# Two-layer adaLN block on one core: float32r products split in parts become plain float32 matmuls

## The chip, the cores and the metric

The kernel runs on one core of a Trainium2 chip. The metric is the device time of one execution in microseconds. Three timed runs of the kernel before took 1040.23, 1040.41 and 1041.82 us, so the median is 1040.41 us.

## The reference

Two layers follow each other on x, two batches of 1024 rows of 128 features. Each layer normalises x, scales and shifts it by a modulation, adds an attention, and then does the same with a feed-forward part. The change touches the second layer alone:

```python
h = layernorm(x) * (1 + ca) + sa
q, k, v = h @ Wq, h @ Wk, h @ Wv              # 128 -> 16 heads of 64
w = softmax(q @ k.T + position_bias)          # 2 batches x 16 heads, 1024 x 1024
x = x + ga * ((w @ v) @ Wo)
h = layernorm(x) * (1 + cb) + sb
for e in range(8):                            # two of eight experts chosen for each row
    inter = h @ wi.T + bi + (h @ lora_A[e].T) @ lora_B[e].T
    out += gate[e] * (relu(inter) @ wo.T + bo)
```

All of it is float32.

## The kernel before

The order of each engine's work is written out by hand; semaphores order the engines against each other. The first layer, its router and its eight experts take the first 200 us and are not touched.

**The second attention.** A unit u is one pair of heads of one batch: 8 pairs x 2 batches = 16 units of 8 tiles. A tile n is 128 query rows of both heads of the pair against 1024 keys; there are 128. Each engine runs through slots n (`pe_slot`, `act_slot`, `dve_slot`, `pool_slot`). In slot n TensorE does:

1. `pe_scores(n + 2)`: query times keys for both heads. The heads lie on partitions 0 to 63 and 64 to 127, so a matmul of one head takes 64 rows of the array and the other head's runs beside it;
2. `pe_turn(n, 0)`: 16 transposes of the softmax of the first head;
3. at most one chunk of the next unit's projections (`pe_chunk`): slots 0 to 3 hold the four chunks of q and k, slots 5 and 7 the two of v, slots 4 and 6 none (unit 1 has its own list, the last unit has four turns of weights instead);
4. `pe_values`: half of a group's product with v. A group is two tiles; the first head goes to partitions 0 to 63 of the bank and the second to 64 to 127, which are two column halves of the array;
5. `pe_turn(n, 1)`: 16 transposes of the second head;
6. in even slots from 4 on `pe_wo`, the output projection of a group.

VectorE adds the position bias to the scores and takes the row bound in one custom instruction for each head (L516), copies the second turn out (L524), and scales the output projection (L533). ScalarE takes the exponentials (L482), copies the first turn out (L474) and each projection chunk (L289, L298). GpSimd adds the result to x (L557, L560).

**The split.** TensorE multiplies q, k and their inputs as float32r (fp32r), one instruction a product. So that the result stays precise, each operand is kept as a high part (its cast to float32r) and a low part (the rest), and each product is made of three matmuls that add up in the bank: high x high, low x high, high x low. This holds for the q and k projections (L354), the scores (L372) and, in the feed-forward part, the products with wi (`base`, L1329) and lora_B (L1363). The parts have to be made:

- h: a cast on ScalarE (L760, `h_high`) and a difference on VectorE (L1045, `split_h`) or, for the second batch, on GpSimd (L710);
- q and k: ScalarE writes `raw_qk`, GpSimd casts (L322) and subtracts (L324); in unit 0 VectorE subtracts (L307);
- the weights: GpSimd (L565, L567);
- the feed-forward part: GpSimd splits its weights (L717, L718) and h (L723, L724), VectorE the low-rank product (L1104) and its masked copies (L1110, L1111).

Every other product is plain float32, which the trace shows as two MATMUL instructions for each matmul of the program (L406: 1024 in the program, 2048 in the trace).

**Getting into the second attention.** The experts' output is gathered in four quarters; VectorE makes x and the normalised rows of each, TensorE turns them (`turn_rows(2, k)`), ScalarE writes `hT`. Unit 0's chunks, and the scores of tiles 0 to 3, are laid between these by hand.

**The feed-forward part** takes 4 steps k of 512 rows: `base` (4 matmuls), two masked products `j` (8 matmuls; 24 instructions as split), the next step's low-rank product and mask turns (`choices`), and 16 output matmuls (L1373).

Of the kernel before, what the change touches and what calls it, by code (L numbers as in the profile page):

```python
# [15 lines left out]
F32R = mybir.dt.float32r  # L16
# [48 lines left out]
def build(nc, rel_hot, L0_attn_x, L0_attn_Wq, L0_attn_bq, L0_attn_Wk, L0_attn_bk, L0_attn_Wv, L0_attn_bv,  # L65
# [4 lines left out]
    with ExitStack() as ctx:  # L70
# [18 lines left out]
        h_high = sb("h_high", [P, N], F32R)  # L89
        h_low = sb("h_low", [P, N], F32R)  # L90
        h_parts = (h_high, h_low)
# [7 lines left out]
        w_parts = sb("w_parts", [P, 2, 2, CK], F32R)  # L99
# [8 lines left out]
        raw_qk = sb("raw_qk", [P, 2, CK])  # L108
        wo_out = sb("wo_out", [P, 2, 2, 2, D])
        qk0 = sb("qk0", [P, 4, S], F32R)  # L110
        with nc.sbuf_tensor("probsT", [P, 2, 2, TB, P], F32) as probsT:
            pass
        qk1 = sb("qk1", [P, 4, S], F32R)
        qk = (qk0, qk1)
        V1 = sb("V1", [P, 2, TB, P])
        wpair = sb("wpair", [P, 2, 3, P])
        wsplit = sb("wsplit", [P, 2, 2, 2, P], F32R)
# [38 lines left out]
        h_ffn = [qk0[:, 0:2, :].rearrange("p a n -> p (a n)"), qk0[:, 2:4, :].rearrange("p a n -> p (a n)")]  # L156
        lowrank = [part(h_high, 0, 512), part(h_high, 512, 512)]
        masked = h_low[:, :].rearrange("p (j a n) -> p j a n", j=2, a=2)

        passes = ((0, 0), (1, 0), (0, 1))  # L160
# [121 lines left out]
        def act_chunk(act, u, c):  # L282

            kind, q = chunk_of(u, c)
            act.wait_ge(ev("proj_full"), 6 * u + c + 1)
            if kind == "v":
                if u >= 2:
                    act.wait_ge(ev("pv_done"), 4 * (u - 1))
                act.copy(V1[:, u % 2, 4 * q:4 * q + 4, :].rearrange("p t d -> p (t d)"), chunk_bank(u, c)).then_inc(ev("high_out"), 1)  # L289
                return  # L290
            sign = -1.0 if kind == "q" else 1.0
            if u == 0:
                act.mul(qk[0][:, 0 if kind == "q" else 2, q * CK:(q + 1) * CK], chunk_bank(u, c), sign).then_inc(ev("high_out"), 1)
                return

            if 4 * u + c >= 6:
                act.wait_ge(ev("low_out"), 4 * u + c - 1)
            act.mul(raw_qk[:, c % 2, :], chunk_bank(u, c), sign).then_inc(ev("high_out"), 1)  # L298

        def dve_chunk(dve, u, c):  # L300

            kind, q = chunk_of(u, c)
            if kind == "v":
                return
            k = 0 if kind == "q" else 2
            dve.wait_ge(ev("high_out"), 6 * u + c + 1)
            dve.scalar_tensor_tensor(out=qk[u % 2][:, k + 1, q * CK:(q + 1) * CK], in0=chunk_bank(u, c),  # L307
                                     scalar=-1.0 if kind == "q" else 1.0,
                                     in1=qk[u % 2][:, k, q * CK:(q + 1) * CK].bitcast(F32),
                                     op0=ALU.mult, op1=ALU.subtract).then_inc(ev("low_out"), 1)  # L310

        def pool_chunk(pool, u, c):

            kind, q = chunk_of(u, c)
            if kind == "v":
                return
            k = 0 if kind == "q" else 2
            at = slice(q * CK, (q + 1) * CK)
            pool.wait_ge(ev("high_out"), 6 * u + c + 1)
            if u >= 2:  # L320
                pool.wait_ge(ev("scores"), 2 * TB * (u - 1))
            pool.tensor_copy(qk[u % 2][:, k, at], raw_qk[:, c % 2, :]).then_inc(ev("qk_high"), 1)  # L322
            pool.wait_ge(ev("qk_high"), 4 * (u - 1) + c + 1)
# [522 lines left out]
        def _(dve):  # L846
# [207 lines left out]
            for c in range(2):  # L1054
                dve_chunk(dve, 0, c)
# [345 lines left out]
```

## Time and profile before

| | |
|---|---|
| median of the three timed runs | 1040.41 us |
| the profiled execution | 1039.06 us |
| its span from first to last instruction | 1037.3 us |
| TensorE matmul busy | 934.1 us, 90% |
| VectorE busy | 668.4 us, 64% |
| ScalarE busy | 590.0 us, 57% |
| GpSimd busy | 281.7 us, 27% |

Busy time counts the union of an engine's instructions. Matmuls are pipelined: the recorded length of one is longer than the time until the next can start, so what a stage costs TensorE is read from the starts. The span is the profiled execution's own time less 1.76 us that lie around it.

### The profile page before, as it was taken

Reading aid. Unit: us, or ns where it says so; the run is one execution under the profiler, and the core shown is the slowest. Engines: PE = TensorE matmul, PEld = TensorE weight load, DVE = VectorE, ACT = ScalarE, POOL = GpSimd, SP = SyncE. Lnnn points to the kernel's source line nnn. Section 1 sums busy time; section 2 is a strip of 40 time slices with the busy share of each in tenths; the row PEclk is TensorE's granted clock in tenths of the full one; section 3 lists DMA queues with packets and bytes.
Section 4 is the critical chain, followed back from the end, with each engine's and each line's share of the span. In section 5 each row is a group of like instructions: output and inputs, shape, how many; then the busy total and the mean of one; then the engine's idle time right before and its main releaser. Section 6 shows DMA issues by size and latency. Waiting matters only on the chain. (4 is left out here: it accounts for less than half of the span.)

```text
span 1037.3 us, 24542 instructions
## 1 busy us (share of the span) xinstructions
PE 934.1 (90%) x9958; PEld 687.5 (66%) x9958; DVE 668.4 (64%) x1352; ACT 590.0 (57%) x980; POOL 281.7 (27%) x332
## 2 busy tenths in 40 slices
PE   7888349457999999999999999999999999996897
PEld 6467338345777777677777767777777776774786
DVE  6277401285767777677677777667777776774665
ACT  2533113236666766766766676676667667672343
POOL 1100540332341422324233142333414233112300
PEclk9999769767999999999999999999999999999999
DMA  8301231100002002000200200110020010000000
GB/s 260 109 1 73 94 89 31 56 23 1 2 2 85 2 2 86 2 2 2 85 3 1 86 2 2 42 46 3 2 85 2 2 37 3 1 3 2 1 21 21
DMA packets 27124, 35.43 MB, mean 34 GB/s; under 512 B 6042, under 2 KB 21716, under 8 KB 26836
## 3 DMA queue, kind: packets, MB, share of 16 engines
q1 hardware_dynamic: 25988, 31.76, 9.2%
q0 software_dynamic: 1024, 2.10, 0.7%
q8 instruction: 80, 1.31, 0.5%
q14 instruction: 32, 0.26, 0.1%
HBM read 28.48 MB, written 5.37 MB: 33 GB/s over the span
## 5 line engine op out<-in xcount | busy, mean ns | idle before, releaser
L516 DVE CUSTOM_DVE_ANT_0 soft<-SC,strips 128x1024 f32<-128x1024 f32 x256 | 303.2, 1221 | 21.1 <-PE SC L372 21.1
L482 ACT ACTIVATE soft<-soft,nmax 128x1024 f32<-128x1024 f32 x256 | 294.0, 1149 | 2.8 <-DVE nmax L516 2.8
L524 DVE COPY PTs<-PT 128x1024 f32<-128x1024 f32 x128 | 156.8, 1225 | 186.0 <-PE PT L390 186.0
L474 ACT COPY PTs<-PT 128x1024 f32<-128x1024 f32 x128 | 129.8, 1014 | 223.9 <-PE PT L390 223.9
L406 PE MATMUL CX<-PTs,V 128*64 128x256 f32 x2048 | 250.7, 387 | 5.7 <-DVE wo_out L533 4.3
L372 PE MATMUL SC<-qk 64*128 64x512 f32 x1536 | 212.4, 409 | 10.4 <-DVE nmax L516 7.0
L390 PEld LDWEIGHTS PT<-ident,soft 64*128 64x128 f32 x4096 | 155.6, 139 | 86.5 <-issue 75.6
L406 PEld LDWEIGHTS CX<-PTs,V 128*64 128x64 f32 x2048 | 136.7, 137 | 89.7 <-issue 24.6
L390 PE MATMUL PT<-ident,soft 64*128 64x64 f32 x4096 | 180.1, 228 | 3.7 <-DVE PTs L524 2.4
L372 PEld LDWEIGHTS SC<-qk 64*128 64x128 f32 x1536 | 137.1, 188 | 35.5 <-issue 4.7
L557 POOL TENSOR_TENSOR x<-x,wo_out 128x256 f32<-128x256 f32 x64 | 47.1, 736 | 259.3 <-DVE wo_out L533 259.3
L322 POOL CAST qk<-raw_qk 128x512 fp32r<-128x512 f32 x60 | 36.8, 614 | 225.1 <-ACT raw_qk L298 225.1
L324 POOL TENSOR_TENSOR qk<-raw_qk,qk 128x512 fp32r<-128x512 f32 x60 | 77.5, 1292 | 4.8
L354 PE MATMUL MI<-h_high,wsplit 128*128 128x512 f32 x122 | 55.6, 455 | 2.9 <-DVE h_low L1045 2.9
L482 ACT ACTIVATION_READ_ACCUMULATOR soft<-soft,nmax 128x1 f32 x256 | 49.3, 193 | 0.0
L806 ACT ACTIVATE probsT<-SC,cols 128x384 f32<-128x384 f32 x32 | 18.6, 581 | 53.9 <-PE SC L1280 52.4
L560 POOL TENSOR_TENSOR x<-x,wo_out 128x256 f32<-128x256 f32 x64 | 47.5, 742 | 5.0
L425 PE MATMUL CX<-wog,ctxs 64*128 64x128 f32 x256 | 42.4, 286 | 0.5 <-ACT ctxs L505 0.5
L425 PE MATMUL MI<-wog,ctxs 64*128 64x128 f32 x256 | 42.4, 286 | 0.0
L1130 PE MATMUL SC<-ident 128*128 128x128 f32 x110 | 17.4, 316 | 24.9 <-DMA slots_in<-probsT,arena 24.9
L841 ACT ACTIVATE probsT<-SC,cols 128x512 f32<-128x512 f32 x32 | 21.9, 690 | 28.2 <-PE SC L1363 28.1
L298 ACT ACTIVATE raw_qk<-MI 128x512 f32<-128x512 f32 x60 | 35.2, 587 | 0.0
(235 smaller groups left out, 1041.4 us busy)
## 6 DMA issues: line engine op xcount, KB each, us to landing
strips<-bias_vec SPq DMA_DIRECT2D x8, 1920.0 KB, 7.1
arena<-in_L_ffn_w SPq DMA_DIRECT2D x1, 2048.0 KB, 10.4
slots_in<-arena SPq DMA_DIRECT2D x1, 1536.0 KB, 9.1
arena<-slots_in SPq DMA_DIRECT2D x8, 192.0 KB, 3.9
slots_out<-arena SPq DMA_DIRECT2D x8, 192.0 KB, 2.0
x<-in_L_attn_x SPq DMA_DIRECT2D x2, 512.0 KB, 4.6
out<-x SPq DMA_DIRECT2D x4, 256.0 KB, 2.3
arena<-in_L_wmod SPq DMA_DIRECT2D x2, 384.0 KB, 5.6
```

The lines of the kernel that those rows point to most:

```text
L324: pool.tensor_tensor(qk[u % 2][:, k + 1, at], raw_qk[:, c % 2, :], qk[u % 2][:, k, at].bitcast(F32), ALU.subtract).then_inc(ev("low_out"), 1)
L354: ins = pe.matmul(bank, wsplit[:, p % 2, wp, "qk".index(kind), :], rhs, start=(n == 0), stop=(n == 2))
L372: ins = pe.matmul(SC[hd][:, k * CK:(k + 1) * CK], qk[u % 2][mine, qp, i * P:(i + 1) * P], qk[u % 2][mine, kp, k * CK:(k + 1) * CK], start= ...
L390: ins = pe.transpose(PT[r][:, t * DK:(t + 1) * DK], soft[mine, n % RING, hd, t * P:(t + 1) * P], ident[mine, mine])
L406: ins = pe.matmul(CX[hd * DK:(hd + 1) * DK, 0:2 * P], V1[:, vb, t, hd * DK:(hd + 1) * DK], PTs[:, g % 2, hd, t, :], start=(t == 0), stop=( ...
L425: ins = pe.matmul(dst, ctxs[mine, g % 4, t * P:(t + 1) * P], wog[mine, u % B, u // B, :], start=(hd == 1 or (g == GROUPS - 1 and t == 0)), ...
L474: act.copy(turned_out(n, 0), turned_in(0)).then_inc(ev("ptA_out"), 1)
L482: act.activation(soft[:, n % RING, hd, :], soft[:, n % RING, hd, :], ACT.Exp, bias=nmax[:, j:j + 1], scale=-1.0, accum_out=rsum[:, hd, n % ...
L516: dve.tensor_tensor_reduce(soft[:, n % RING, hd, :], SC[hd][:, :], strips[:, u // B % 2, hd, i * P:i * P + S], 1.0, 3.4e38, ALU.add, ALU.m ...
L524: dve.tensor_copy(turned_out(n, 1), turned_in(1)).then_inc(ev("ptB_out"), 1)
L557: pool.tensor_tensor(x[:, t0:t0 + 2, :], x[:, t0:t0 + 2, :], wo_out[:, g % 2, 1, :, :], ALU.add).then_inc(ev("x_half"), 1)
L560: pool.tensor_tensor(x[:, t0:t0 + 2, :], x[:, t0:t0 + 2, :], wo_out[:, g % 2, 0, :, :], ALU.add).then_inc(ev("x_added"), 1)
```

## The change

Everything that was float32r becomes float32, and the parts go away: three matmuls of high and low parts become one float32 matmul with the unsplit operands. In the projections of the second attention each matmul is given as two with half of the output columns each (for v, half of the rows of h), which land on partitions 0 to 63 and 64 to 127 of the bank. The casts and differences on ScalarE, VectorE and GpSimd are gone; ScalarE writes q and k where TensorE reads them. VectorE's slot -1 is moved ahead of the second batch's rows.

```diff
@@ act_chunk
-            act.mul(raw_qk[:, c % 2, :], chunk_bank(u, c), sign).then_inc(ev("high_out"), 1)
+            if u >= 2:
+                act.wait_ge(ev("scores"), 2 * TB * (u - 1))
+            act.mul(qk[u % 2][:, "qk".index(kind), q * CK:(q + 1) * CK], chunk_bank(u, c),
+                    -1.0 if kind == "q" else 1.0).then_inc(ev("chunk_out"), 1)
@@ dve_chunk, pool_chunk, pool_split, split_h and their calls
- (gone)
@@ pe_chunk, v
-                    ins = pe.matmul(bank[:, t * P:(t + 1) * P], hT[:, ...], wpair[:, p % 2, 2, :], start=True, stop=True)
+                    for r in range(2):
+                        at = b * S + (4 * q + t) * P + r * DK
+                        ins = pe.matmul(bank[r * DK:(r + 1) * DK, t * P:(t + 1) * P], hT[:, at:at + DK],
+                                        wpair[:, p % 2, 2, :], start=True, stop=True)
@@ pe_chunk, q and k
-                for n, (hp, wp) in enumerate(((0, 0), (1, 0), (0, 1))):
...
-                    ins = pe.matmul(bank, wsplit[:, p % 2, wp, "qk".index(kind), :], rhs, start=(n == 0), stop=(n == 2))
+                for r in range(2):
+                    mine = slice(r * DK, (r + 1) * DK)
+                    pe.matmul(bank[mine, :], wpair[:, p % 2, "qk".index(kind), mine], rhs,
+                              start=True, stop=True).then_inc(ev("proj_full"), 1)
@@ pe_scores
-                for m, (qp, kp) in enumerate(((0, 2), (0, 3), (1, 2))):
-                    for hd in range(2):
...
-                        ins = pe.matmul(SC[hd][...], qk[u % 2][mine, qp, ...], qk[u % 2][mine, kp, ...], start=(m == 0), stop=(m == 2))
+                for hd in range(2):
+                    mine = slice(hd * DK, hd * DK + DK)
+                    ins = pe.matmul(SC[hd][...], qk[u % 2][mine, 0, ...], qk[u % 2][mine, 1, ...], start=True, stop=True)
@@ norm_out
-                        act.wait_ge(ev("hT_ready"), 4 * n + k + 1)
-                        act.copy(h_high[:, at], hT[:, at]).then_inc(ev("h_high"), 1)
@@ vector
             norm_variance(2, 1)
             dve_slot(dve, -2)
+            dve_slot(dve, -1)
             norm_rows(2, (1,))
-            for n in range(-1, TILES + 4):
+            for n in range(TILES + 4):
@@ vector, feed-forward part
-                tt(lowrank[1], MI[:, :], lowrank[0].bitcast(F32), ALU.subtract).then_inc(ev("low_split"), 1)
-                    tt(masked[:, j, 0, :], PT[j][:, :], lowrank[0].bitcast(F32), ALU.mult)
-                    tt(masked[:, j, 1, :], PT[j][:, :], lowrank[1].bitcast(F32), ALU.mult).then_inc(ev("masked"), 1)
+                    tt(masked[:, j, :], PT[j][:, :], lowrank, ALU.mult).then_inc(ev("masked"), 1)
@@ tensor, into the second attention
-            pe.wait_ge(ev("h_split"), 1)
+            pe.wait_ge(ev("hT_ready"), 9)
...
-            pe.wait_ge(ev("h_split"), 4)
@@ tensor, feed-forward part
-                pe.wait_ge(ev("ffn_h_split"), k + 1)
-                    for n, (wp, hp) in enumerate(passes):
-                        mm(four_sc[c], w_parts[:, 0, wp, ...], h_ffn[hp][...], start=(n == 0), stop=False, ...)
+                    mm(four_sc[c], wT[:, WI + c, :], hT[:, k * 512:(k + 1) * 512], start=True, stop=False, ...)
-                        for m, (wp, hp) in enumerate(passes):
-                            ins = mm(four_sc[c], w_parts[:, 1, wp, ...], masked[:, j, hp, :], start=False, stop=(m == 2), ...)
+                        mm(four_sc[c], wT[:, LB + c, :], masked[:, j, :], start=False, stop=True, ...)
```

## Rows read from the trace of the kernel before

**Rows 1.** The page's 40 slices of the span: TensorE's busy tenths and granted clock.
```profile
PE   7888349457999999999999999999999999996897
PEclk9999769767999999999999999999999999999999
```

**Rows 2.** Timeline of TensorE, a slot pair: start us, us, what.
```profile
605.65 1.64 PE L372 MATMUL SC<-qk 64*128 64x512 f32 x12
607.28 0.72 PE L390 MATMUL PT<-ident,soft 64*128 64x64 f32 x16
607.92 0.50 PE L354 MATMUL MI<-h_high,wsplit 128*128 128x512 f32 x1
...
608.82 1.95 PE L406 MATMUL CX<-PTs,V 128*64 128x256 f32 x16
610.70 0.71 PE L390 MATMUL PT<-ident,soft 64*128 64x64 f32 x16
...
611.52 0.27 PE L425 MATMUL CX<-wog,ctxs 64*128 64x128 f32 x1
611.53 0.27 PE L425 MATMUL MI<-wog,ctxs 64*128 64x128 f32 x1
611.63 0.27 PE L425 MATMUL CX<-wog,ctxs 64*128 64x128 f32 x1
...
611.67 1.63 PE L372 MATMUL SC<-qk 64*128 64x512 f32 x12
613.14 0.65 PE L390 MATMUL PT<-ident,soft 64*128 64x64 f32 x16
```

**Rows 3.** The same timeline, a slot with a chunk of v.
```profile
624.19 1.16 PE L347 MATMUL MI<-wpair,hT 128*128 128x128 f32 x8
625.27 1.95 PE L406 MATMUL CX<-PTs,V 128*64 128x256 f32 x16
```

**Rows 4.** Timeline of all engines: VectorE's copy of the second turn.
```profile
605.90 1.23 DVE L524 COPY PTs<-PT 128x1024 f32<-128x1024 f32 x1 [1.56 <-PE PT L390]
```

**Rows 5.** The chain that ended last, feed-forward step: start us, us, what.
```profile
999.43 0.86 PE MI L1340 x2
...
1001.16 3.61 PE CX L1373 x32
...
1007.53 5.49 PE SC L1363 x24
```

**Rows 6.** Timeline of all engines on the way into the second attention.
```profile
210.98 0.62 ACT L760 CAST h_high<-hT 128x512 fp32r<-128x512 f32 x1
212.23 0.69 DVE L1045 TENSOR_TENSOR h_low<-hT,h_high 128x512 fp32r<-128x512 f32 x1
212.98 0.80 PE L354 MATMUL PT<-h_high,wsplit 128*128 128x512 f32 x1 [2.84 <-DVE h_low L1045]
...
228.52 1.23 DVE L516 CUSTOM_DVE_ANT_0 soft<-SC,strips 128x1024 f32<-128x1024 f32 x1
...
236.41 2.09 PE L372 MATMUL SC<-qk 64*128 64x512 f32 x12 [2.44 <-DVE nmax L516]
...
246.93 2.93 PE L372 MATMUL SC<-qk 64*128 64x512 f32 x12 [3.33 <-POOL h_low L710]
```

**Rows 7.** Timeline of all engines ahead of the feed-forward part.
```profile
947.34 0.17 DVE L885 TENSOR_TENSOR st<-st 128x8 f32<-128x8 f32 x1
...
948.19 2.14 DVE L890 TENSOR_SCALAR probs<-x,mv,st 128x128 f32<-128x128 f32 x8
...
961.25 0.72 DVE L885 TENSOR_TENSOR st<-st 128x8 f32<-128x8 f32 x1
...
963.01 4.12 DVE L890 TENSOR_SCALAR probs<-x,mv,st 128x128 f32<-128x128 f32 x8
...
966.16 0.65 PE L1160 MATMUL SC<-ident,probs 128*128 128x128 f32 x4 [2.14 <-DVE probs L890]
...
980.08 5.75 PE L1363 MATMUL SC<-h_low,w_parts 128*128 128x512 f32 x24 [1.16 <-DVE h_low L1111]
```

More of the change, by code:

```diff
@@ L107, in build @@
         probs = sb("probs", [P, 2, S])
[L108 to L114, printed above, removed]
+        qk0 = sb("qk0", [P, 2, S])
+        probsT = sb("probsT", [P, 2, 2, TB, P])
+        qk1 = probsT[:, 1, :, :, :].rearrange("p h k q -> p h (k q)")
+        qk = (qk0[:, :, :], qk1)
         V1 = sb("V1", [P, 2, TB, P])
         wpair = sb("wpair", [P, 2, 3, P])
-        wsplit = sb("wsplit", [P, 2, 2, 2, P], F32R)
         strips = sb("strips", [P, 2, 2, STRIP])
@@ L155, in build @@
         gbb = part(flat, 27 * P, E)
[L156 to L160, printed above, removed]
+        lowrank = qk0[:, 0, 0:512]
+        masked = qk0[:, 1, :].rearrange("p (j n) -> p j n", j=2)
         hot_wide = part(flat, 0, 8 * P).rearrange("p (j t d) -> p j t d", j=2, t=4)
@@ L288, in act_chunk @@
                     act.wait_ge(ev("pv_done"), 4 * (u - 1))
-                act.copy(V1[:, u % 2, 4 * q:4 * q + 4, :].rearrange("p t d -> p (t d)"), chunk_bank(u, c)).then_inc(ev("high_out"), 1)
+                act.copy(V1[:, u % 2, 4 * q:4 * q + 4, :].rearrange("p t d -> p (t d)"), chunk_bank(u, c)).then_inc(ev("chunk_out"), 1)
                 return
[L291 to L297, printed above, removed]
-            act.mul(raw_qk[:, c % 2, :], chunk_bank(u, c), sign).then_inc(ev("high_out"), 1)
[L300 to L319, printed above, removed]
-            if u >= 2:
-                pool.wait_ge(ev("scores"), 2 * TB * (u - 1))
-            pool.tensor_copy(qk[u % 2][:, k, at], raw_qk[:, c % 2, :]).then_inc(ev("qk_high"), 1)
-            pool.wait_ge(ev("qk_high"), 4 * (u - 1) + c + 1)
-            pool.tensor_tensor(qk[u % 2][:, k + 1, at], raw_qk[:, c % 2, :], qk[u % 2][:, k, at].bitcast(F32),
-                               ALU.subtract).then_inc(ev("low_out"), 1)
+            if u >= 2:
+                act.wait_ge(ev("scores"), 2 * TB * (u - 1))
+            act.mul(qk[u % 2][:, "qk".index(kind), q * CK:(q + 1) * CK], chunk_bank(u, c),
+                    -1.0 if kind == "q" else 1.0).then_inc(ev("chunk_out"), 1)
         def pe_chunk(pe, u, c):
@@ L331, in pe_chunk @@
             if c == 0 and b == 0:
-                pe.wait_ge(ev("w_split"), p + 1)
+                pe.wait_ge(ev("ld_pair"), 48 * p + 48)
+            if c == 0 and u == 1:
+                pe.wait_ge(ev("hT_ready"), 12)
             bank = chunk_bank(u, c)
@@ L572, in pool_slot @@
                 pool_add(pool, (n - 5) // 2)
-            what, a, c = middle(n)
-            if what == "chunk":
-                pool_chunk(pool, a, c)
-            if n % (B * TB) == 4 and n // (B * TB) + 1 < PAIRS:
-                pool_split(pool, n // (B * TB) + 1)
         block = ctx.enter_context(nc.Block())
@@ L1051, in _ @@
             quarter_variance(1)
-            split_h(0)
             quarter_rows(1)
-            for c in range(2):
-                dve_chunk(dve, 0, c)
             gathered(2)
-            split_h(1)
-            for c in range(3, 5):
-                dve_chunk(dve, 0, c)
             gathered(3)
```

98 lines of the change are left out of this document (29 added, 69 removed).

## The prediction

> **What bounds the kernel now.** I read the 40 slices first: from slice 10 to slice 37 TensorE is busy at nine tenths or more at full granted clock [rows 1]. Those are the 128 tiles of the second attention. The timeline of TensorE then shows that in this stretch its units follow each other with no gap that another engine explains, bar one [rows 2]. A slot with a q or k chunk and an output projection takes 611.67 - 605.65 = 6.02 us, and what the slot is made of is read from starts: scores 607.28 - 605.65 = 1.63, first turn 0.64, chunk 608.82 - 607.92 = 0.90, values 610.70 - 608.82 = 1.88. The next slot's scores take only 613.14 - 611.67 = 1.47 with the same 12 instructions. The missing 0.16 us is the one gap: where no output projection stands between the second turn and the scores, the first turn has to wait for VectorE's copy of the second, which runs from 605.90 to 607.13, until 607.28 [rows 2, 4]. So the stretch is bound by TensorE's streaming, and 0.16 us of cover exists in every other slot. Ahead of it and behind it, chains through several engines decide [rows 6, 7].
>
> **What a matmul costs here.** The chain of the feed-forward part gives the pace, since nothing else ends there. 24 float32r instructions of 512 columns take 5.49 us, so 0.23 us each. Two float32 instructions (one matmul of the program) of 512 columns take 0.86, so 0.43 each; 32 of 128 columns take 3.61, so 0.11 each [rows 5]. A float32 matmul of 512 columns is thus 0.86 us against 3 x 0.23 = 0.69 us for the split one. Do two halves of the array still run beside each other in float32? By rows: at L425, the pair of the two heads, 64 rows each, starts at 611.52 and 611.53 and the next pair 0.11 us later, as fast as one full-array instruction of 128 columns. By columns: values, 16 instructions of 256 columns in 1.88 us, are 8 pairs of 0.235, where 256 columns cost 0.43 / 2 = 0.215 in one half alone [rows 2, 5]. Both pair.
>
> **Scores.** Twelve float32r instructions in 6 pairs are 6 x 0.23 = 1.38 us, which with 0.09 at the edge is the 1.47 seen. After: 4 matmuls, 8 instructions, 4 pairs of 0.43 = 1.72. That is +0.34 us. In slots behind an output projection all of it is on the path: 1.81. In the others 0.16 is covered by the copy that the turn waits for anyway: 1.81 - 1.63 = +0.18. Of the 124 tiles after the way in, half are of each kind: 62 x 0.34 + 62 x 0.18 = +32 us. No row shows a 512-column row pair in float32. The lower bound is 1.72 with the edge hidden (-0.09 a tile, -11 us); the upper is that such a pair, streaming two inputs, keeps the 0.015 us by which float32r at 0.23 exceeds the 0.215 of half a float32 instruction, for each of its two sweeps: +0.03 x 4 a tile, +15 us. I take 0.43, since the 128-column pair pays nothing.
>
> The Trainium skill, FP8 and Floating Point Precision, section TensorE Precision Notes, says that true FP32 takes four passes through the array. Were each pass priced as a float32r instruction is here, scores would be 8 x 0.23 = 1.84 and not 1.72, which is the upper bound above, reached by another way.
>
> **Projections.** A q or k chunk takes 0.90 now [rows 2]. After: two column halves of one float32 matmul, 2 pairs x 0.43 = 0.86. Values pay 1.88 - 8 x 0.215 = 0.16 for entering and leaving the column split; as values follow the chunk and are split the same way, part is shared. So 0.86 to 1.02; I take 0.91. A v chunk takes 625.27 - 624.19 = 1.08 now [rows 3], after 8 pairs of 0.11 = 0.90 to 1.06; I take 0.95. Over 15 units: 15 x (4 x 0.01 - 2 x 0.13) = -3 us, bounds -8 and +7. ScalarE's writing of q and k only changes its target; its new wait, for the scores of the unit before last, is over a slot earlier. SP's wait for the projections keeps its place.
>
> The Trainium skill, TensorE: Matmul & The Clock Gate, Part 3, "The mechanism", says that weight loads overlap running matmuls only when the row groups differ. Column halves share their rows, so by that rule their loads would stand open; the row of values, 16 loads in 1.88 us, does not bear it out.
>
> **GpSimd and the casts.** 60 casts and 60 differences leave GpSimd, which bounds nothing in the slots; I take 0 for that, and nothing is late next as its additions to x finish well inside two slots.
>
> **The way in.** Three waits of TensorE for parts of h go. Before the first chunks it starts at 212.98, while `hT` is there when ScalarE's cast begins, at 210.98: 2.0 us of the wait. Chunks 3 and 4 stand behind the same two steps: about 2.0 again. Before tile 3's scores it waits 3.33 us for GpSimd's two differences, until 246.93. VectorE loses six instructions of 0.69 us, 4.1 us in all [rows 6]. I followed the timeline with these taken out; what comes out are estimates. VectorE's first bias instruction moves from 228.52 to where its work on the last gathered quarter can end, about 222.7. Scores and bias then alternate: tile 2's scores go from 236.41 to 229.6 at the full clock or 231.3 at the half one, tile 3's from 246.93 to between 235.5 and 240.3, now behind the turned rows. That is -11.4 to -6.6, and -5.6 if the slower tile 3 is itself at the half clock. The granted clock flips in this stretch [rows 1], so I take the middle, -8.5 us. What is late next is VectorE's order of bias and rows.
>
> **The feed-forward part.** Here each step is TensorE's alone [rows 5]. The masked products: 16 instructions of 0.43 = 6.88 for 5.49, +1.4 in each of 4 steps, +5.5 us. `base`: 8 x 0.43 = 3.44 for 12 x 0.23 = 2.76, +0.7 in three (the first lies beside VectorE's routing): +2.0. Back: the second batch's rows took 4.12 us on VectorE against 2.14 for the same eight instructions of the first batch, and a small one before them (L885) 0.72 against 0.17, while GpSimd was splitting weights and h; TensorE waited for them [rows 7]. That is 2.5, and with a second small one like it -2.9. And one difference and one masked copy on VectorE, of 512 columns like the 0.69 at 212.23 [rows 6], go from between the low-rank product and the first masked matmul, where the mask's turns cover a part; 980.08 becomes about 979.3: -0.8. Sum +3.8, bounds +2 and +7.
>
> **Sum.** +32 - 3 - 8.5 + 3.8 = +24.3 us. Span 1037.3 + 24.3 = 1061.6; with the 1.76 around it 1063.4. The profiled execution lies 1.35 below the median of the runs, so 1064.7 us.
>
> **Rivals.**
> 1. A pass keeps float32r's price (the upper bound above): scores +47 instead of +32, chunks +0.06 each and the feed-forward part +2 more: 1064.7 + 15 + 3 + 2 = 1085. For it: every float32r row reads 0.23. Against: every float32 row is at its own pace. 8%.
> 2. The column halves run one after the other: 4 x 0.43 = 1.72 for a q or k chunk, 1.8 for v. 15 x (4 x 0.81 + 2 x 0.85) = +74, so 1139. For it: both halves stream the same h, which no row shows. Against: values pair with shared rows. 6%.
> 3. Not slower: the slots turn out to be held by the loop of turn, copy and turn in all slots, not in every other one, so that longer scores fill a wait. It decides from 0.34 us of wait in each slot; then the scores cost 0 and the time is 1064.7 - 32 = 1033. For it: the 0.16 us. Against: the 1.47 us slots hold six pairs at full pace. 4%.
> 4. The change does not do what it says: float32 operands compiled to one instruction each, which would be far faster. Every float32 row of this kernel has two. Under 1%.
>
> My forecast has the remaining 81%. The range takes the forecast's bounds of scores, chunks and way in, not all at one end: 1054 to 1080. A difference of 0.2%, 2 us, is about what can be told from no change. Faster 0.04, same 0.02, slower 0.94.
>
> **What would show it.** Scores to first turn 1.80 us in all slots, none at 1.63; a q or k chunk 0.91 and v 0.95; slots of 6.2 and 5.7 us for the pair above; tile 3's scores at about 239; a feed-forward step of 15.6 us for 13.6; the second batch's L890 rows at 2.1 us. If chunks are 1.7 rival 2 holds; if scores are above 1.88, rival 1. It would be wrong if the copy wait moved along with the scores.

## The result and the profile after

The changed kernel takes 1049.43 us (median of four runs, 1048.81 to 1054.29) against 1040.32 for the kernel before: a ratio of 1.0097 [1.0069, 1.0124]. (This ratio and those below are estimated over all runs of both kernels, here with a fifth run of 1051.04 us; the two medians alone give 1.0088.) It is slower, as forecast, but by 9 us instead of 24, and the time lies below the range of 1054 to 1080. The profiled execution took 1054.29 us (span 1052.5) and is the longest of the set, so stages are compared below, not spans.

The page of the changed kernel: TensorE's busy tenths and granted clock in 40 slices (it stands against [rows 1]).

```profile
PE   7888449469999999999999999999999999996997
PEclk8899769779999999999999999999999999998999
```

The timeline of TensorE over a slot pair, as [rows 2], and a slot with a chunk of v, as [rows 3]. L336 is the scores, L354 the turns, L318 a q or k chunk, L370 values, L389 the output projection, L307 the v chunk.

```profile
601.42 1.88 PE L336 MATMUL SC<-qk 64*128 64x512 f32 x8
603.14 0.66 PE L354 MATMUL PT<-ident,soft 64*128 64x64 f32 x16
603.73 1.08 PE L318 MATMUL MI<-hT,wpair 128*64 128x512 f32 x4
604.64 1.90 PE L370 MATMUL CX<-PTs,V 128*64 128x256 f32 x16
606.47 0.71 PE L354 MATMUL PT<-ident,soft 64*128 64x64 f32 x16
607.01 1.94 PE L336 MATMUL SC<-qk 64*128 64x512 f32 x8
608.78 0.66 PE L354 MATMUL PT<-ident,soft 64*128 64x64 f32 x16
...
612.66 0.33 PE L389 MATMUL CX<-wog,ctxs 64*128 64x128 f32 x1
...
613.16 1.88 PE L336 MATMUL SC<-qk 64*128 64x512 f32 x8
...
626.35 1.09 PE L307 MATMUL MI<-wpair,hT 128*64 128x128 f32 x16
627.27 1.03 PE L370 MATMUL CX<-PTs,V 128*64 128x256 f32 x8
```

From start to start: scores 1.72 behind an output projection and 1.77 elsewhere, first turn 0.59 everywhere, q or k chunk 0.91, v chunk 0.92, values 604.64 to 606.47 = 1.83 (1.88 before), output projection 0.50 (0.42 before). The slots are 5.59 us (601.42 to 607.01) and 6.15 (607.01 to 613.16); they were 5.35 and 6.02.

The timeline of the way into the second attention, as [rows 6]: ScalarE's first `hT`, TensorE's first chunks, VectorE's first bias instruction, and the scores of tiles 2, 3 and 4.

```profile
212.68 0.78 ACT L685 ACTIVATE hT<-SC,modc 128x512 f32<-128x512 f32 x1 [3.52 <-PE SC L1073]
213.51 2.83 PE L318 MATMUL PT<-hT,wpair 128*64 128x512 f32 x6 [0.87 <-ACT hT L685]
...
225.00 1.22 DVE L480 CUSTOM_DVE_ANT_0 soft<-SC,strips 128x1024 f32<-128x1024 f32 x1
...
231.94 2.73 PE L336 MATMUL SC<-qk 64*128 64x512 f32 x8 [2.43 <-DVE nmax L480]
...
239.69 2.06 PE L336 MATMUL SC<-qk 64*128 64x512 f32 x8
...
244.31 1.99 PE L336 MATMUL SC<-qk 64*128 64x512 f32 x8
```

In this execution the first gather starts 2.56 us later than before (199.28 against 196.72), a start that lies between 194.3 and 199.5 in all the profiles, whichever kernel ran. Taken off, VectorE's first bias instruction stands at 222.4 (222.7 forecast, 228.52 before) and tile 3's scores at 237.1. The first of these is luck of this one execution: counted from the first gather, the first bias stands at 25.7 us here, but at 30.8, 31.2 and 32.0 in the three other profiles with the same start (e1, e12, e5), and at 31.8 to 36.2 in the five that start as the kernel before.

The timeline of VectorE ahead of the feed-forward part, as [rows 7]: the normalised rows of both batches.

```profile
959.00 2.14 DVE L817 TENSOR_SCALAR probs<-x,mv,st 128x128 f32<-128x128 f32 x8
...
973.49 2.14 DVE L817 TENSOR_SCALAR probs<-x,mv,st 128x128 f32<-128x128 f32 x8
```

The chain that ended last, the feed-forward steps, as [rows 5]: L1269 the masked products, L1238 `base`.

```profile
987.74 7.13 PE SC L1269 x16
...
1000.22 3.44 PE SC L1238 x8
1003.65 6.87 PE SC L1269 x16
...
1015.87 3.44 PE SC L1238 x8
```

One step is 1015.87 - 1000.22 = 15.65 us (13.59 before, 15.6 forecast).

To compare kernels I cut every profiled execution at three starts read from its timeline. "Way in" runs from the first of the 16 gathers behind the first layer to tile 4's scores, the "tiles" from there to tile 127's scores, the "end" from there to the last instruction. A unit is eight slots, the mean of twelve.

| kernel | way in | tiles | unit | end | timed ratio to before |
|---|---|---|---|---|---|
| before | 55.7 | 676.3 | 44.07 | 108.5 | 1 |
| the changed kernel | 45.0 | 695.0 | 45.28 | 113.2 | 1.0097 [1.0069, 1.0124] |
| e1_after_again | 47.7 | 695.0 | 45.28 | 113.2 | 1.0114 [1.0084, 1.0143] |
| e2_full_width | 48.3 | 713.2 | 46.51 | 112.6 | 1.0271 [1.0235, 1.0306] |
| e3_scores_only | 55.8 | 704.0 | 45.88 | 110.5 | 1.0238 [1.0198, 1.0279] |
| e4_ffn_only | 57.7 | 676.4 | 44.07 | 112.3 | 1.0027 [1.0005, 1.0048] |
| e5_gpsimd_load | 48.9 | 695.0 | 45.28 | 116.9 | one run |
| e6_old_order | 51.2 | 695.0 | 45.28 | 113.4 | one run |
| e7_twice_even | 61.2 | 678.6 | 44.22 | 110.4 | 1.0021 [0.9992, 1.0049] |
| e8_twice_odd | 60.8 | 690.8 | 45.03 | 108.9 | 1.0137 [1.0091, 1.0182] |
| e9_split_scores | 51.1 | 667.9 | 43.52 | 113.2 | 0.9884 [0.9860, 0.9908] |
| e10_split_masked | 51.0 | 667.7 | 43.50 | 108.4 | 0.9807 [0.9782, 0.9832] |
| e11_before_again | 58.4 | 676.4 | 44.07 | 108.6 | one run |
| e12_after_third | 48.1 | 695.0 | 45.28 | 113.5 | one run |

The tiles repeat within 0.1 us for the same code. The way in scatters, and so does the stretch ahead of it: the start of the first gather moves by 5.2 us from profile to profile and is in none of the three stages.

### The profile page after: what moved, and what is told of

It is laid out like the page before. It is cut to its first block and busy times, and to the rows that moved or that the text cites. A ratio compares the mean times of both kernels' runs of the same rounds, so it can differ in the third digit from the quotient of the medians.

```text
span 1052.5 us, 23827 instructions
## 1 busy us (share of the span) xinstructions
PE 961.7 (91%) x9718; PEld 617.8 (59%) x9718; DVE 656.3 (62%) x1334; ACT 587.6 (56%) x976; POOL 143.5 (14%) x182
## 5 line engine op out<-in xcount | busy, mean ns | idle before, releaser
L370 PE MATMUL CX<-PTs,V 128*64 128x256 f32 x2048 | 246.5, 383 | 5.7 <-DVE wo_out L497 4.3
L354 PEld LDWEIGHTS PT<-ident,soft 64*128 64x128 f32 x4096 | 161.0, 139 | 118.4 <-issue 91.2
L370 PEld LDWEIGHTS CX<-PTs,V 128*64 128x64 f32 x2048 | 143.4, 137 | 98.5 <-issue 36.8
L354 PE MATMUL PT<-ident,soft 64*128 64x64 f32 x4096 | 176.7, 226 | 3.8 <-DVE PTs L488 2.4
L336 PE MATMUL SC<-qk 64*128 64x512 f32 x512 | 123.5, 601 | 4.6 <-DVE nmax L480 4.5
L336 PE MATMUL SC<-probsT 64*128 64x512 f32 x512 | 122.3, 596 | 0.0
L318 PE MATMUL MI<-hT,wpair 128*64 128x512 f32 x244 | 65.8, 618 | 0.9 <-ACT hT L685 0.9
L336 PEld LDWEIGHTS SC<-qk 64*128 64x128 f32 x512 | 44.5, 189 | 37.2 <-issue 33.1
L336 PEld LDWEIGHTS SC<-probsT 64*128 64x128 f32 x512 | 44.3, 188 | 30.4 <-issue 30.4
L389 PE MATMUL CX<-wog,ctxs 64*128 64x128 f32 x256 | 42.6, 287 | 0.5 <-ACT ctxs L469 0.5
L389 PE MATMUL MI<-wog,ctxs 64*128 64x128 f32 x256 | 42.6, 287 | 0.0
L389 PEld LDWEIGHTS CX<-wog,ctxs 64*128 64x128 f32 x256 | 34.2, 191 | 1.7 <-ACT ctxs L469 1.3
```

The costliest lines, as they stand in the source:

```text
L318: pe.matmul(bank[mine, :], wpair[:, p % 2, "qk".index(kind), mine], rhs, start=True, stop=True).then_inc(ev("proj_full"), 1)
L336: ins = pe.matmul(SC[hd][:, k * CK:(k + 1) * CK], qk[u % 2][mine, 0, i * P:(i + 1) * P], qk[u % 2][mine, 1, k * CK:(k + 1) * CK], start=Tr ...
L354: ins = pe.transpose(PT[r][:, t * DK:(t + 1) * DK], soft[mine, n % RING, hd, t * P:(t + 1) * P], ident[mine, mine])
L370: ins = pe.matmul(CX[hd * DK:(hd + 1) * DK, 0:2 * P], V1[:, vb, t, hd * DK:(hd + 1) * DK], PTs[:, g % 2, hd, t, :], start=(t == 0), stop=( ...
L389: ins = pe.matmul(dst, ctxs[mine, g % 4, t * P:(t + 1) * P], wog[mine, u % B, u // B, :], start=(hd == 1 or (g == GROUPS - 1 and t == 0)), ...
```

## The experiments

### The change again, and with the projections at full width

> The changed kernel once more, to have a second trace of it beside its timed runs. Theory: its first profile was long by what lies ahead of the second attention and in the clock of the way in, not by the slots. Then a unit of eight slots takes 45.3 us again, tile 4's scores start 8 to 10 us ahead of the kernel before by the same start of the gathers, and the time is 1049 to 1050 us, +9. Rival: the slots themselves vary from run to run; then a unit reads another length than 45.3.

Measured: 1054.22 us (six runs, 1051.3 to 1056.9) against 1042.49 for the kernel before on that chip, +11.7 us; tiles and unit are the same to 0.01 us. The time misses the 1049 to 1050 us of the theory; the slots do not vary, so the rival is out.

In the changed kernel, each projection matmul is given once over the whole array again:

```diff
-                for r in range(2):
-                    mine = slice(r * DK, (r + 1) * DK)
-                    pe.matmul(bank[mine, :], wpair[:, p % 2, "qk".index(kind), mine], rhs,
-                              start=True, stop=True).then_inc(ev("proj_full"), 1)
+                pe.matmul(bank, wpair[:, p % 2, "qk".index(kind), :], rhs,
+                          start=True, stop=True).then_inc(ev("proj_full"), 1)
@@ v likewise; the waits for proj_full count one instead of two
```

> The changed kernel with its projections as single full-width float32 matmuls, no column halves. Theory (edges): the halves save the passage from one tiling of the array to another; without them a q or k chunk takes 1.05 us and not 0.91, a v chunk 1.09 and not 0.92, and the values behind a chunk 1.88 and not 1.83, so 15 x (4 x 0.14 + 2 x 0.17 + 6 x 0.05) = +18 us on the changed kernel. Rival (streaming alone counts): two halves of 0.43 side by side are worth one full matmul of 0.43, so no difference over 2 us.

Measured: 1071.95 us, 1.0271 [1.0235, 1.0306]; the tiles take 18.2 us more than with halves. Timeline of TensorE in it: a slot with v, then one with q or k (L306 v, L314 q and k, L366 values).

```profile
604.55 1.16 PE L306 MATMUL MI<-wpair,hT 128*128 128x128 f32 x8
605.64 1.95 PE L366 MATMUL CX<-PTs,V 128*64 128x256 f32 x16
607.52 0.71 PE L350 MATMUL PT<-ident,soft 64*128 64x64 f32 x16
...
610.43 1.13 PE L314 MATMUL MI<-hT,wpair 128*128 128x512 f32 x2
611.49 1.95 PE L366 MATMUL CX<-PTs,V 128*64 128x256 f32 x16
613.37 0.71 PE L350 MATMUL PT<-ident,soft 64*128 64x64 f32 x16
```

The same arithmetic takes 1.06 instead of 0.91 for q and k, 1.09 instead of 0.92 for v, and the values behind either take 1.88 instead of 1.83. The two float32 instructions of a q or k chunk stream for 0.86 at the pace of [rows 5]; 0.20 is then paid around them, against 0.05 in column halves. So what halves save is no streaming but a part of the passage from row halves (turns) over the full array to column halves (values). The turn ahead of the chunk takes 0.59 either way, so the saving lies in the chunk and behind it. The timeline of the weight loads (PEld) of the values shows where, in this kernel and then in the changed one:

```profile
611.49 0.63 PEld L366 LDWEIGHTS CX<-PTs,V 128*64 128x64 f32 x8 [0.76 <-issue]
```

```profile
604.21 0.14 PEld L370 LDWEIGHTS CX<-PTs,V 128*64 128x64 f32 x2 [0.29 <-issue]
```

Behind a full-width chunk the values' first loads start at 611.49, together with their first matmul. Behind a chunk in column halves they start at 604.21, 0.43 us ahead of the first matmul (604.64) and beside the chunk's last pair. Whether it is the open load or the change of tiling itself that costs the time, no run takes apart. The halves of the array do run side by side: one after the other a q or k chunk would take 1.72.

The Trainium skill, TensorE: Matmul & The Clock Gate, Part 3, "The mechanism", states that weight loads overlap running matmuls only when the row groups differ. The load at 604.21 does not agree with that: it runs beside the chunk's last pair of matmuls, over the same rows. Nor does the v chunk in column halves, whose 16 matmuls and 16 loads over the same rows take 0.92 us in all.

### One part alone: scores, feed-forward part

In the kernel before, only the scores become one float32 matmul, and q and k stay unsplit:

```diff
-                for m, (qp, kp) in enumerate(((0, 2), (0, 3), (1, 2))):
+                for m, (qp, kp) in enumerate(((0, 1),)):
@@ act_chunk writes qk unsplit; dve_chunk and pool_chunk are gone
```

> The kernel before with the scores alone in plain float32; projections and the feed-forward part stay split. Theory (the term for scores was right, the miss lies in the edges of other units): scores 1.81 us in all slots, the first turn behind them 0.59 for 0.65 where it waited, v chunks 1.08 and values 1.88 as before, a unit 44.1 + 2.0 - 0.2 = 45.9 us, +28 us over the stretch and +24 to +30 on the kernel before. Rival (the pairs of 512 columns or the cover were cheaper than priced, and that is the miss): a unit at 45.2, +17 to +20.

Measured: 1065.91 us, 1.0238 [1.0198, 1.0279]; tiles +27.6 us against before. Timeline of TensorE in it, a slot of the kind that waited for VectorE's copy before (L369 scores, L387 turns, L349 the chunk, L403 values):

```profile
605.94 1.94 PE L369 MATMUL SC<-qk 64*128 64x512 f32 x8
607.72 0.66 PE L387 MATMUL PT<-ident,soft 64*128 64x64 f32 x16
608.30 0.50 PE L349 MATMUL MI<-h_high,wsplit 128*128 128x512 f32 x1
...
609.21 1.95 PE L403 MATMUL CX<-PTs,V 128*64 128x256 f32 x16
611.08 0.71 PE L387 MATMUL PT<-ident,soft 64*128 64x64 f32 x16
```

Scores 1.77, first turn 0.59 (0.64 before), values 1.87. A pair of slots costs 0.45 us more than before (unit 45.88 for 44.07), where I had 0.34 + 0.18 = 0.52. The time, +23.4 us, ends just under the theory's +24 to +30; the unit is the 45.9 of the theory. The changed kernel's tiles are 9.0 us shorter than these, and the two differ over the tiles by the projections alone: that is what the column halves bring next to float32 scores.

In the kernel before, only the feed-forward part becomes plain (GpSimd's splits, VectorE's difference and one masked copy gone):

```diff
-                    for n, (wp, hp) in enumerate(passes):
-                        mm(four_sc[c], w_parts[:, 0, wp, ...], h_ffn[hp][...], start=(n == 0), stop=False, ...)
+                    mm(four_sc[c], wT[:, WI + c, :], hT[:, k * 512:(k + 1) * 512], start=True, stop=False, ...)
@@ the masked products likewise
```

> The kernel before with the feed-forward part alone in plain float32, its splits on GpSimd and VectorE gone. Theory: step 15.65 us for 13.59, the second batch's eight rows on VectorE 2.1 us for 4.1, together +4 to +5 us. Rival (VectorE was slow there for another reason than GpSimd's work): the rows stay at 4.1 and the kernel loses +7.

Measured: 1044.86 us against 1042.49, 1.0027 [1.0005, 1.0048]; the end is 3.8 us longer, the tiles unchanged. That is the forecast's +3.8, and just under the +4 to +5 written ahead of this run. Its parts hold too: the first masked product starts 47.50 us behind tile 127's scores and not 51.31, so 3.8 come back (forecast 3.7), and the masked products and `base` then cost 7.6 (forecast 7.5).

### What slowed VectorE, and what its order is worth

The changed kernel with GpSimd's splits of the weights and of h put back; their results go to a spare buffer that nobody reads:

```diff
+            for k in range(4):
+                pool.wait_ge(ev("hT_ready"), 12 + k + 1)
+                at = slice(k * 512, (k + 1) * 512)
+                link(pool.tensor_copy(spare[:, 0, :], hT[:, at]))
+                link(pool.tensor_tensor(spare[:, 1, :], hT[:, at], spare[:, 0, :].bitcast(F32), ALU.subtract))
@@ and two such pairs for the weights ahead of it
```

> The changed kernel with GpSimd again doing the casts and differences of the feed-forward part (weights and h) at the same place, into a spare tile that nobody reads or waits for. Theory: VectorE and GpSimd share something on the way to SBUF, and the second batch's eight row instructions were slow for that: they go from 2.14 back to about 4.1 us, the tail after the last scores from 113.2 to 115.5 to 116.2. Rival: VectorE was slow because of the chain it sits in; then 2.14 stays and the tail is 113.2.

Measured: the end is 116.9 us, 3.7 longer than without this load and over the 115.5 to 116.2 of the theory. Timeline of VectorE and GpSimd in it, and under it the same rows L830 queried in a short window (count, shortest, median and longest in ns, first and last start):

```profile
971.72 1.64 DVE L817 BATCH_NORM_STATS2 bst<-x 128x6 f32<-128x128 f32 x8 [1.31 <-POOL x L526]
...
972.32 1.27 POOL L665 TENSOR_TENSOR spare<-strips,spare 128x512 fp32r<-128x512 f32 x1
...
976.39 1.26 POOL L670 TENSOR_TENSOR spare<-hT,spare 128x512 fp32r<-128x512 f32 x1
976.61 4.42 DVE L830 TENSOR_SCALAR probs<-x,mv,st 128x128 f32<-128x128 f32 x8
977.71 0.61 POOL L669 CAST spare<-hT 128x512 fp32r<-128x512 f32 x1
978.40 1.26 POOL L670 TENSOR_TENSOR spare<-hT,spare 128x512 fp32r<-128x512 f32 x1
```

```profile
L830 DVE TENSOR_SCALAR probs<-x,mv,st x2: 749/1086/1424, 977.7 to 978.3; 128x128 f32<-128x128 f32 x2
```

The eight rows take 4.42 us again (4.12 in [rows 7], 2.14 in the changed kernel). The slow ones go on when GpSimd's end: GpSimd's instructions end at 977.65, 978.32 and 979.66, VectorE's second and third rows start at 977.65 and 978.33 in the trace and the fourth at 979.67. After that each takes its 0.34 us. That GpSimd's work slows VectorE is shown by this run; that VectorE stands still until GpSimd's instruction is over, and does not just run slower, is read from these equal times. The small instructions between the statistics and the rows lose another 0.9 us (3.21 for 2.27 from the first BATCH_NORM_AGGREGATE to the first row), which the theory had left out.

The Trainium skill, SBUF — State Buffer, section "SBUF: two separate sides", describes a port pair that VectorE and GpSimd share as a lock held for a whole instruction, so that the loser fully blocks. These rows agree with that. The page also says that whoever starts first gets it, and that these rows do not show: the two later GpSimd instructions are recorded 0.06 to 0.08 us behind the VectorE instruction that waits for them.

The changed kernel with VectorE's slot -1 back behind the second batch's rows:

```diff
-            dve_slot(dve, -1)
             norm_rows(2, (1,))
-            for n in range(TILES + 4):
+            for n in range(-1, TILES + 4):
```

> The changed kernel with VectorE's slot -1 back behind the second batch's rows, as before the change. Theory: of the 8 to 10 us won on the way in, the rows' 3.3 us are in front of tile 1's bias again and tile 2's scores start 3 us later, but the rows stood between tile 1's and tile 2's bias otherwise, so tile 3 and 4 lose under 1 us: the order moves the wait and wins little, and the gain is the removed parts. Rival: the order is half of the gain; tile 4's scores start 3 to 4 us later from the first gather than 45.0 to 47.7.

Measured: a way in of 51.2 us, where the changed kernel has 45.0, 47.7 and 48.1, and e5, with the same start, 48.9. Most of the difference is not the order's. VectorE's slot -1 comes behind tile 0's scores, and tile 0's scores already stand 29.6 us behind the first gather here (23.2, 27.9, 28.0 and 29.6 in the four others). From tile 0's to tile 4's scores this kernel takes 21.6 us, the four others 21.8, 19.8, 20.1 and 19.3. What can be put down to the order is 0.9 us: tile 2's scores follow tile 1's after 5.33 us and not 4.42, with the rows between the two bias instructions. The theory's 3 us at tile 2 do not show, but its conclusion holds: the order wins little. Tile 4's scores do start 3.5 to 6.2 us later than the 45.0 to 47.7 of the rival, but that was made almost wholly ahead of the place where the order can act.

### How much cover the copy gave

In the kernel before, a seventh pair of float32r matmuls of the high parts goes ahead of the scores' six, in even tiles only (the slots whose turn waits for the copy), or in odd ones only (`n % 2 == 1`). The scores overwrite what it wrote.

```diff
+            if n >= 6 and n % 2 == 0:
+                for hd in range(2):
+                    mine = slice(hd * DK, hd * DK + DK)
+                    pe.matmul(SC[hd][:, 0:CK], qk[u % 2][mine, 0, i * P:(i + 1) * P],
+                              qk[u % 2][mine, 2, 0:CK], start=True, stop=True)
```

> The kernel before, with the first float32r pair of the scores issued twice in each even tile from 6 on: 61 times 0.23 us more TensorE work, in the slots where the first turn waits for VectorE's copy. Nothing of the result changes. Theory (cover): 0.16 us is hidden and the turn behind it is 0.06 shorter once it no longer waits, so a unit reads 44.07 + 4 x 0.01 = 44.1 to 44.3 and the time grows by 0 to 4 us. Rival (no cover; the edge is TensorE's own): +0.93 a unit, +14 us. The tile's number decides which slots these are: if the even tiles are the ones behind an output projection, this run and the next change places.

> The same with the odd tiles from 7 on. Theory: behind an output projection the turn does not wait, all 0.23 us count, a unit reads 44.07 + 4 x 0.23 = 45.0 and the time grows by 14 us. Rival (cover everywhere, or none anywhere): the same growth as for the even tiles.

Measured: 61 more pairs in even tiles cost 2.2 us over the tiles, 0.04 each (ratio 1.0021 [0.9992, 1.0049]); in odd tiles 14.5 us, 0.24 each (1.0137 [1.0091, 1.0182]). Timeline of TensorE in the kernel with even pairs, a waiting slot:

```profile
612.24 0.48 PE L371 MATMUL SC<-qk 64*128 64x512 f32 x2
612.55 1.56 PE L377 MATMUL SC<-qk 64*128 64x512 f32 x12
613.94 0.66 PE L395 MATMUL PT<-ident,soft 64*128 64x64 f32 x16
614.54 0.50 PE L354 MATMUL MI<-h_high,wsplit 128*128 128x512 f32 x1
```

Seven pairs take 1.70 us where six and the wait took 1.63, and the turn behind them 0.60 where it took 0.64. So of the pair's 0.24 us all but 0.04 was hidden: the cover is 0.20 us, not the 0.16 that I read from the scores alone. The rest sits inside the turn, which took 0.64 where it followed the wait and takes 0.60 without one.

### Keeping what gains and undoing what loses

The changed kernel with q and k split again (GpSimd's `pool_chunk` and VectorE's `dve_chunk` of unit 0 are back) and the scores of three float32r matmuls:

```diff
-                for hd in range(2):
-                    ins = pe.matmul(SC[hd][...], qk[u % 2][mine, 0, ...], qk[u % 2][mine, 1, ...], start=True, stop=True)
+                for m, (qp, kp) in enumerate(((0, 2), (0, 3), (1, 2))):
+                    for hd in range(2):
+                        ins = pe.matmul(SC[hd][...], qk[u % 2][mine, qp, ...], qk[u % 2][mine, kp, ...], start=(m == 0), stop=(m == 2))
```

> The changed kernel with one part undone: q and k are split into two float32r parts again (GpSimd makes them, VectorE in unit 0) and the scores are three float32r matmuls of each kind; the projections in column halves, the start's order and the plain feed-forward stay. Theory (the scores alone carry the loss over the stretch; of the rest the column halves take v chunk 1.09 to 0.92 us twice a unit and the values behind a chunk 1.88 to 1.83 us six times a unit): the unit comes from 44.07 us before to 43.4, so the stretch is 10 us shorter than before; the start is 5 to 8 us shorter than before; the end 4 us longer. Sum: 10 to 14 us under the kernel before, a ratio of 0.987 to 0.990. Rival A (the column halves only win next to plain scores, since the passage between a score tiling and theirs decides): unit 44.0 to 44.1, the whole 2 to 5 us under the kernel before. Rival B (the start's gain came from the missing GpSimd and VectorE steps of unit 0, not from the halves): start 0 to 2 us shorter, the whole 6 to 8 us under.

Measured: 1030.62 us against 1043.29, 0.9884 [0.9860, 0.9908], as the theory's range for the whole. The tiles are 8.4 us shorter, not 10: the unit is 43.52, since q and k chunks are 0.01 to 0.02 longer each, and so are the turns ahead of them that follow an output projection (0.60 for 0.58). Timeline of TensorE in it (L344 v, L406 values):

```profile
612.27 0.65 PE L390 MATMUL PT<-ident,soft 64*128 64x64 f32 x16
612.85 1.09 PE L344 MATMUL MI<-wpair,hT 128*64 128x128 f32 x16
613.78 1.90 PE L406 MATMUL CX<-PTs,V 128*64 128x256 f32 x16
615.61 0.71 PE L390 MATMUL PT<-ident,soft 64*128 64x64 f32 x16
```

A v chunk of 0.93 and values of 1.83, next to float32r scores too: the halves need no float32 scores to gain, so rival A is out. The way in, 51.1, lies between the 45 to 49 of the changed kernel's start and the 56 to 61 of the kernel before's; part of its gain hung on the splits of q and k, as rival B says, and part did not.

The same kernel with the masked products split again as well, the split of their weights moved into an early slot:

```diff
+                if n == TILES:
+                    pool.wait_ge(ev("wT_ready"), 4)
+                    full = wT[:, LB:LB + FC, :].rearrange("p c d -> p (c d)")
+                    link(pool.tensor_copy(lb_parts[:, 0, :], full))
+                    pool.tensor_tensor(lb_parts[:, 1, :], full, lb_parts[:, 0, :].bitcast(F32), ALU.subtract).then_inc(ev("lb_split"), 1)
@@ VectorE's difference and second masked copy are back; three passes for each masked product
```

> As the kernel with split scores, and the masked product of the feed-forward is three float32r passes again, its weights split by GpSimd in an early slot of the second attention instead of beside the feed-forward's beginning; base and low-rank product stay plain. Theory (the plain masked product costs 5.5 us over the four steps, the plain base costs 2.0, and what VectorE gains ahead of the feed-forward, rows of 0.34 us instead of up to 1.42, comes from GpSimd doing nothing beside it and not from the plain arithmetic): the end is 1 us shorter to 0.5 us longer than before, against 4 longer in the kernel with split scores; the whole is 14 to 18 us under the kernel before, ratio 0.983 to 0.987. Rival (VectorE's two more products and the subtraction in each step stand on the path of a step and cost as much as TensorE's passes save): the end stays 3 to 5 us longer than before and this kernel takes the time of the one with split scores.

Measured: 1023.98 us (five runs, 1022.93 to 1024.34) against 1043.29, 0.9807 [0.9782, 0.9832], faster than both kernels; the theory's 0.983 lies at the upper end of the interval. The chain that ended last in it (L1293 `base`, L1327 masked products):

```profile
974.44 3.44 PE SC L1293 x8
977.88 5.47 PE SC L1327 x24
...
988.70 3.44 PE SC L1293 x8
```

A masked product of three float32r passes takes 5.47 us against 6.87 in float32, the step is 14.26 instead of 15.65, and the end is 108.4 us, as before, though `base` is plain. The stages account for 13.5 us of the gain (55.7 to 51.0, 676.3 to 667.7, 108.5 to 108.4); the timed 19.3 is 6 us more. But 55.7 is the shortest way in of its kind; with the mean of 58.8 found below, the stages give 16.5. The remaining 3 us lie within the scatter of what stands ahead of the gathers; no profile here shows which stage they are. The end is in the theory's range, so the rival is out.

### Does the way in scatter?

> The kernel before once more, for a second profile of its way into the second attention. Theory (the way in is the part of the run that scatters, since the granted clock falls and rises in it, while the slots repeat to a hundredth of a microsecond): from the first gather to tile 4's scores between 55 and 62 us, with the half clock in other places than in the first profile, and the stretch of tiles at 676.3 us again, the end at 108 to 109. Rival (the slots scatter too): a stretch that differs by over 1 us from 676.3 and a way in of 55 to 57.

> The changed kernel a third time, on the same chip as the kernel before. Theory (the way in scatters, and is 10 to 11 us shorter than before's in the mean, not 8.5): from the first gather to tile 4's scores 45 to 49 us, the stretch 695.0, the end 113.2. Rival (the gain of the start is 8.5 us as forecast and the kernel before's profile was typical): a way in of 47 to 50 us next to one of 55 to 57 in the kernel before.

Measured: way in 58.4 and 48.1, tiles 676.4 and 695.0, end 108.6 and 113.5. The kernels that start as the kernel before (it twice, e4, e7, e8) have 55.7, 58.4, 57.7, 61.2 and 60.8, a mean of 58.8; those that start as the changed one (it three times, e5) 45.0, 47.7, 48.1 and 48.9, a mean of 47.4 (e2, e3, e6, e9 and e10 start in ways between the two and are left out). The windows of the way in (us, each engine's busy time and instructions, granted clock, DMA share, GB/s), of the kernel before, of its second profile, and of the changed kernel:

```profile
196.70:252.40 55.70, 25.83 (x158) 19.44 (x160) 34.16 (x109) 20.52 (x33) 18.72 (x18) 0.63 0.07 21
```

```profile
195.00:253.40 58.40, 26.84 (x160) 20.11 (x161) 33.89 (x109) 20.67 (x33) 18.03 (x18) 0.60 0.08 20
```

```profile
199.30:244.30 45.00, 25.00 (x164) 13.28 (x165) 30.12 (x104) 18.50 (x30) 15.91 (x16) 0.70 0.09 26
```

The chip may play a part in the scatter. The two kernels with the old start that ran on the same chip have 61.2 and 60.8, and taken chip by chip the gain is 10.0 (e4 and e1), 12.1 (e7, e8 and e5), 10.3 (e11 and e12) and 10.7 us in the first two profiles.

The way in can be cut once more, at tile 0's scores. Ahead of them the old start takes 27.1 to 31.4 us and the new one 23.2 to 29.6: that is where most of the scatter lies, and the means differ by 2.3. From tile 0's to tile 4's scores the old start takes 28.6 to 29.8 and the new one 19.3 to 21.8: there lie 9.0 of the 11.3 us. Three parts of these 9.0 can be named. From tile 2's to tile 3's scores, where TensorE waited 3.33 us for GpSimd's difference of h [rows 6], the old start takes 10.5 to 11.0, e3, which keeps that split, 10.9, and e9 and e10, which do not, 6.5 and 6.7: about 4 us. The splits of q and k, which e9 and e10 have again, are about 3.3 (23.6 and 23.5 from tile 0 to tile 4, 20.3 in the mean without them). The order is 0.9.

A mean granted clock of 0.63 and 0.60 before, 0.70 after: TensorE stands more than half of this stretch idle in the kernel before, and the chip grants the lower level, 1.2 GHz, for more of it. Tile 3's scores stood in it in both profiles of the kernel before, 2.93 us long [rows 6] where the slots' are 1.63 [rows 2].

## Why the forecast was right in sign and wrong in size

The sum, term by term, in us (a gain is negative):

| term | forecast | measured | from |
|---|---|---|---|
| scores | +32 | +27.6 | e3 against before, tiles |
| projections | -3 | -9.0 | changed kernel against e3, tiles |
| way in | -8.5 | -11.3 | the two means |
| feed-forward part | +3.8 | +4.7 | end; e4 alone +3.8 |
| sum | +24.3 | +12.0 | timed +9.1 and +11.7 |

**The pace and the pairing: right.** Row pairs of 512 float32 columns stream at 0.43, four of them in 1.72, with no price for the second stream; 1.84 appears nowhere, so rival 1 fell. Column halves pair (0.91, not 1.72), so rival 2 fell. Rival 3 was half seen and half missed: the tiles became 19 us longer, so nothing covers all slots, but the cover is larger than I gave it.

**Scores: mechanism right, term too large by 4.4.** Behind an output projection I had +0.34; the scores rose by 0.25, since their edge of 0.09 is gone, and the output projection ahead of them by 0.08, since that edge moved there: 0.33. In the waiting slots I had +0.18. Scores +0.14, turn -0.05 and the second turn ahead +0.03 make about +0.12. The step that failed here is "0.16 is covered": I took the wait from the scores' start-to-start time and not from the turn as well, which read 0.64 in these slots and 0.58 in the others. E7 measured the cover at 0.20.

**Projections: the mis-sized term.** The step that failed is "as values follow the chunk and are split the same way, part is shared". I gave the shared passage to the chunk only, and too little of it. A v chunk became 0.92 and not 0.95, and the values behind every chunk fell from 1.88 to 1.83, six times a unit, which I had not counted. In 15 units: 15 x (2 x -0.17 + 6 x -0.05 + 4 x 0.01) = -9.0. The bound of -8 would nearly have held it. That the halves' gain can outlive the chunk is read from e2: behind a full-width chunk the values take their 1.88 again, and their first loads no longer start ahead.

**Way in: direction right, price low, one step right by luck.** The forecast was made at tile 3's scores. There the two means of the time from the first gather, 52.9 and 42.9 us, differ by 10.0, for -8.5; the other 1.3 lie between tile 3's and tile 4's scores, which I had not priced. VectorE's first bias came where I had put it in one profile; over all of them it moved by 4.3 us and not 5.8. And I subtracted from one profile that was the shortest of five. The total of -11.3 is at the edge of the bounds of -11.4 to -5.6. The step that held is the wait for GpSimd's part of h ahead of tile 3's scores: 3.33 us of wait, 4 us gone.

**Feed-forward part: right.** Step 15.65 for 15.6, rows 2.14 for 2.1, and e5 shows that the 4.12 us of [rows 7] came from GpSimd. E4 alone gives +3.8. Of the changed kernel's further 0.9, 0.25 are tile 127's own scores (1.72 for 1.47). The other 0.7 are the last group's values, which take 3.68 us at a mean granted clock of 0.62 around them, for 3.01 at 0.76 in e4. That is not the change's: e9, with float32r scores, has it as well and the same end of 113.2.

**The range.** The misses of scores (-4.4), projections (-6.0) and way in (-2.8) all point down, and are what carried the time out of the range. I had set the range by taking bounds "not all at one end"; they came out near one end together. Two of the three are one reading error: edges between stages were held fixed, while the change moved them.

Still open: stages give +12.0 where the two sets of runs gave +9.1 and +11.7, a difference within the 5.2 us by which the first gather's start moves; the way in has only four or five profiles on a side; and what makes the part ahead of tile 0's scores scatter is not shown.

## What to carry to other kernels

Price a change of a TensorE stage together with the stage behind it: where neighbouring stages use other parts of the array, giving the middle one the tiling of its successor saved 0.20 us a chunk (0.22 for v) with the same arithmetic, and 18 us in all. When a wait stands ahead of a step, read the step's own length too before calling the cover. Where a part of the timeline runs at a changing granted clock, take it from more than one profile, and undo the parts of a mixed change one by one: here undoing two parts turned +9 us into -19.

## What the runs showed of the hardware that I had not expected

- The passage over the full array between row halves and column halves costs 0.20 us more than the one with a chunk in column halves (1.06 + 1.88 against 0.91 + 1.83), though both ways stream the same columns. In the two places looked at, the loads of the stage behind start 0.43 us ahead of its first matmul where the tiling stays (604.21), and together with it where the tiling changes (611.49).
- VectorE's instruction that normally takes 0.34 us took up to 1.42 us beside GpSimd's two-input ones, and the next one started within 0.01 us of their end; its statistics (BATCH_NORM_STATS2, one operand) beside the same load kept their 1.64 us for eight, as in the changed kernel without the load.
- With the same start the way in repeats only within 4 to 6 us (45.0 to 48.9, 55.7 to 61.2), while the 123 tiles behind it repeat within 0.1 us. Most of that scatter lies ahead of tile 0's scores.
